# Position table in four rounds of 256 distances, a reordered set-up, and second-layer queries projected in transposed form

## The reference, cut to what matters

```python
# first attention layer
xn = ln(x, g_norm)
q = (xn @ Wq).reshape(b, n, 16, 64).transpose(0, 2, 1, 3)
k, v = split(xn @ Wkv)
k, v = concat(null_kv[0], k), concat(null_kv[1], v)
q, k = l2norm(q) * q_scale, l2norm(k) * k_scale
h = silu(ln(pos @ w0 + b0, g0))        # pos = -n+1 .. n-1
h = silu(ln(h @ w1 + b1, g1))
table = h @ w2 + b2                    # one value for each distance and head
sim = q @ k.T * 8 + table[i - j + n - 1]      # causal, masked
x = x + ln(softmax(sim) @ v @ Wout, g_out)
# second attention layer: no l2norm, scale 1/8, bias read from the input
q = (ln(x, g_in) @ Wq) * 64 ** -0.5
sim = q @ k.T + fside[h, i, j]
x = x + ln(softmax(sim) @ v @ Wo, g_out)
# then two layers: gate, top 2 of 8 experts, two shared experts
logits = (x @ wt.T + (cond @ wg.T)) / 2
```

## Time and profile before

| | us |
|---|---|
| median of the runs | 1698.04 (1697.50 to 1702.49, three runs) |
| the profiled execution, its own time | 1696.38 |
| its span, first to last instruction | 1694.6 |
| PE busy | 1441.5 |
| DVE busy | 1415.4 |
| ACT busy | 1208.0 |
| POOL busy | 775.5 |

### The profile page before, as it was taken

One profiled execution on the slowest core, in us unless ns is written; L12 is line 12 of the kernel. 1 busy time (PEld: TensorE's weight loads), 2 busy tenths in 40 slices (PEclk: granted clock), 3 DMA queues, 4 the chain that ended last, 5 costly groups with the idle time before them and its releaser, 6 DMA issues.

```text
span 1694.6 us, 44574 instructions
## 1 busy us (share of the span) xinstructions
PE 1441.5 (85%) x15543; PEld 1060.4 (63%) x15543; DVE 1415.4 (84%) x3551; ACT 1208.0 (71%) x3063; POOL 775.5 (46%) x1539
## 2 busy tenths in 40 slices
PE   1357777788879999987788888999999989999998
PEld 1245555566667777775566666777777756666665
DVE  4657678888898999986788888899999979888886
ACT  1168788888878999987788888999999923333332
POOL 5657786554444434446664332323222256632222
PEclk9679899999999999998999999999999999999999
DMA  4012121111221123202222121211223001000000
GB/s 141 1 31 63 33 82 51 51 63 64 76 76 67 67 95 111 67 19 59 66 64 68 51 94 70 77 65 72 79 101 130 22 1 44 2 1 1 14 14 26
DMA packets 50496, 96.57 MB, mean 57 GB/s; under 512 B 3396, under 2 KB 27092, under 8 KB 50276
## 3 DMA queue, kind: packets, MB, share of 16 engines
q1 hardware_dynamic: 45568, 90.27, 16.1%
q10 hardware_dynamic: 4708, 3.45, 0.7%
HBM read 91.54 MB, written 2.17 MB: 55 GB/s over the span
## 4 chain that ended last, share of the span: by engine, by line
PE 47%; DVE 19%; ACT 12%; issue 10%; POOL 3%; DMA 1%; DVEq 0%; ACTq 0%; POOLq 0%; SPq 0%
PE tp L1479 7%; DVE p_lo L1105 6%; DVE biased L1019 6%; ACT p_hi L780 5%; PE sc L1186 4%; PE sc L1188 4%; PE sc L1187 4%; PE sc L1373 4%; ACT q_b L709 3%; PE sc L1374 3%; ACT probs L688 2%; PE tp L1186 2%; PE op L1186 2%; PE tp L1187 2%; PE tp L1188 2%
## 5 line engine op out<-in xcount | busy, mean ns | idle before, releaser
L1105 DVE TENSOR_TENSOR p_lo<-tp,p_hi 128x512 f16<-128x512 f32 (+3 forms) x768 | 411.4, 553 | 109.4 <-ACT p_hi L780 102.2
L688 ACT ACTIVATE probs<-biased,neg_max 128x256 f32<-128x256 f32 (+7 forms) x512 | 395.5, 772 | 19.2 <-DVE neg_max L1019 17.8
L1479 PE MATMUL tp<-ident,probs 128*128 128x128 f32 x2304 | 390.3, 279 | 17.9 <-DVE p_lo L1105 16.0
L780 ACT ACTIVATE p_hi<-tp 128x512 f16<-128x512 f32 (+3 forms) x768 | 366.4, 491 | 30.3 <-PE tp L1479 20.8
L1186 PE MATMUL op<-v_s,p_hi 128*128 128x64 f16 x2304 | 285.2, 194 | 55.0 <-DVE p_lo L1105 37.6
L1373 PE MATMUL sc<-k_a,q_a 128*128 128x512 f16 (+3 forms) x768 | 254.3, 331 | 84.1 <-DVE neg_max L1019 75.6
L1479 PEld LDWEIGHTS tp<-ident,probs 128*128 128x128 f32 x2304 | 268.7, 142 | 54.1 <-issue 37.2
L1188 PE MATMUL op<-v_s,p_lo 128*128 128x64 f16 x2304 | 284.2, 194 | 0.0
L1187 PE MATMUL op<-v_s,p_hi 128*128 128x64 f16 x2304 | 284.2, 194 | 0.0
L1186 PEld LDWEIGHTS op<-v_s,p_hi 128*128 128x128 f16 x2304 | 216.2, 99 | 86.9 <-DVE p_lo L1105 62.8
L1374 PE MATMUL sc<-k_b,q_b 128*128 128x512 f16 (+3 forms) x768 | 242.3, 329 | 0.0
(11 more groups left out here) (290 smaller groups left out, 3618.0 us busy)
## 6 DMA issues: line engine op xcount, KB each, us to landing
bias<-rel_table SPq DMA_DIRECT2D x4, 2048.0 KB, 9.0
bias<-in_fside_16xSxS SPq DMA_DIRECT2D x4, 2048.0 KB, 8.3
bias<-rel_table SPq DMA_DIRECT2D x4, 1792.0 KB, 7.3
bias<-in_fside_16xSxS SPq DMA_DIRECT2D x4, 1792.0 KB, 7.6
bias<-rel_table SPq DMA_DIRECT2D x4, 1536.0 KB, 6.2
bias<-in_fside_16xSxS SPq DMA_DIRECT2D x4, 1536.0 KB, 6.5
bias<-rel_table SPq DMA_DIRECT2D x4, 1280.0 KB, 5.6
bias<-in_fside_16xSxS SPq DMA_DIRECT2D x4, 1280.0 KB, 6.1
```

What stands on the lines that cost most here:

```text
L688: ac.activation(probs[:, i % 2, 0:w], biased[:, i % 2, 0:w], ACT.Exp, bias=neg_max[:, u % 2, i % HU:i % HU + 1], scale=-1.0, accum_out=row ...
L780: ac.activation(p_hi[:, gi % 4, 0:nb * P], tp[gi % 2][:, 0:nb * P], ACT.Copy)\
L1105: ve.tensor_tensor(p_lo[:, gi % 4, 0:nb * P], tp[gi % 2][:, 0:nb * P], p_hi[:, gi % 4, 0:nb * P], ALU.subtract).then_inc(s["p_lo"], 1)
L1479: last = te.transpose(tp[gi % 2][:, jj * P:(jj + 1) * P], probs[:, n % 2, (j0 + jj) * P:(j0 + jj + 1) * P], ident[:, :])
```

## The change

Two things are changed together.

The position table is made in four rounds of 256 distances (rounds 0 to 3). Round 0, the distances that tiles 0 and 1 need, is made in slots -18 to -8 (`FILL`). Rounds 1 to 3 are made in slots 0 to 20, 32 to 52 and 64 to 84 (`ROUND`, `ROOTS`), each in small steps inside the attention slots; each writes its quarter of the table, and SP waits for it before the loads of every second tile. The stages are split by operation into `table_stats`, `table_mixed`, `table_scale`, `table_gain`, `table_active` and `table_out` on DVE, `table_tanh` and `table_turned` on ACT, `table_turn` and `table_mix` on PE. What stood before the loop moves into it: x statistics of tile 0 need only x's first tiles, loaded by SP as its first transfer; the null key's products of layer 1 stand at slot -8 behind round 0's table, those of layer 2 are 17 small steps at slots 132 to 148; the gate constants are made at slots 119 and 123 (`PREP`). POOL splits fewer pieces early, in an order that has the first head group first. The null key's logits move from slot 32T-11 to 32T-7, and POOL's null term from unit m+3 to m+2, with two buffers for `q_r`.

In the second layer, queries are projected already transposed: at k = 3, for unit m+2, twelve matmuls of 128 columns with Wq as the fixed operand and x transposed as the moving one. The projection at k = 1, the copy to `q_n` and the two transposes go; the scale moves into the copy to `q_b` and into a scalar_tensor_tensor for the low part.

```diff
-        rh = moe_w[:, 0:2048].rearrange("p (k n) -> p k n", k=TILES)
+        rh = moe_w[:, 0:512].rearrange("p (k n) -> p k n", k=2)
...
-        TABLE_AT = {-17: 4, -15: 5, -14: 6, -10: 7, -8: 8}
+        STATS, SCALE, GAIN, ACTIVE, TURN, MIX, OUT = range(7)
+        FILL = {-18: (STATS, 0), -17: (SCALE, 0), -15: (ACTIVE, 0), -14: (MIX, 0),
+                -10: (SCALE, 1), -9: (ACTIVE, 1), -8: (OUT, 1)}
+        ROUND = {0: (STATS, 0, 0), 1: (STATS, 0, 1), 4: (SCALE, 0, 0), 5: (GAIN, 0, 0), 6: (ACTIVE, 0, 0),
+                 7: (TURN, 0, 0), 8: (MIX, 0, 0), 11: (MIX, 0, 1), 13: (SCALE, 1, 0), 14: (GAIN, 1, 0),
+                 18: (ACTIVE, 1, 0), 19: (TURN, 1, 0), 20: (OUT, 1, 0)}
+        ROOTS = {2: 0, 12: 1}
...
+        PREP = (119, 123)
...
+            sp.dma_start(x_sb[:, :, 0, :], x_in[:, :, 0, :]).then_inc(s_in["x"], 16)
             load_job(sp, 0)
-            load_job(sp, 1)
...
-            write_table(sp)
+            write_table(sp, 0)
             load_bias(sp, 0)
             load_bias(sp, 1)
             n_jobs = 3
             for g in range(2, STEPS * HG):
+                if g % HG == 0 and g <= 3 * HG:
+                    write_table(sp, g // HG)
                 load_bias(sp, g)
...
+            SPLITS = {-17: 2, -16: 2, -15: 2, -13: 1, -9: 1}
...
+                if part == OUT:
+                    table_out(0, sc[1][0:H, 0:2 * P])
+                    null_keys()
...
+            def table_stats(j, i):
+
+                r, half_ = divmod(j, 2)
...
+                    link(ve.scalar_tensor_tensor(rh[:, i, :], rvec[:, 0, :], rel_f[:, k_:k_ + 1], rvec[:, 1, :],
+                                                 ALU.mult, ALU.add))
+                last = ve.bn_stats(r_st[:, i, :], rh[:, i, :])
...
+            def table_scale(j):
+
+                dve.wait_ge(setup["rstd"], j + 1)
+                for i in range(2):
+                    last = ve.tensor_scalar(rh[:, i, :], rh[:, i, :], r_mv[:, i, 0:1], r_rs[:, i:i + 1],
+                                            ALU.subtract, ALU.mult)
+                link(last)
...
+            def table_tanh(j):
+                act.wait_ge(setup["z"], j + 1)
+                ac.activation(re, rh, ACT.Tanh, scale=0.5).then_inc(setup["tanh"], 1)
+
+            def table_turned(j, bank):
+                act.wait_ge(setup["pt"], j + 1)
+                ac.activation(rht.rearrange("p c k n -> p (c k n)"), bank, ACT.Copy).then_inc(setup["t"], 1)
...
+                if k == 3 and U0 <= m + 2 < NU:
+                    u = m + 2
+                    T, hg, bt = u // UNITS, (u % UNITS) // B, u % B
+                    take(False, (s["q_lo"], 2 * (u + 1)))
...
+                    for c in range(UW // P):
+                        cols = slice(hg * UW + c * P, hg * UW + (c + 1) * P)
+                        for kc in range(KC):
+                            last = three(first[:, c * P:(c + 1) * P], wq[1][:, 0, kc, cols], wq[1][:, 1, kc, cols],
+                                         xt[:, T % 2, 0, bt, kc, :], xt[:, T % 2, 1, bt, kc, :],
+                                         kc == 0, kc == KC - 1)
+                    last.then_inc(s["q_t"], 1)
-                if k == 3 and 0 <= m + 2 < NU:
+                if k == 3 and 0 <= m + 2 < U0:
...
-                if k == 1 and 0 <= m + 3 < NU:
+                if k == 1 and 0 <= m + 3 < U0:
```

More of the change, by code:

```diff
@@ L323, in model @@
                 step = min(PIECE, per) if gain is not None else PIECE
-                for c in range(0, size, step):
+                starts = list(range(0, size, step))
+                if gain is not None:
+                    starts.sort(key=lambda c: (c % per, c // per))
+                for c in starts:
                     w = min(step, size - c)
@@ L770, in small @@
                                       ACT.Copy).then_inc(s["ot_hi"], 1)
+                    r, step_ = in_round(n, ROUND)
+                    if r and step_[0] == GAIN:
+                        table_tanh(2 * r + step_[1])
+                    if r and step_[0] == TURN:
+                        table_turned(2 * r + step_[1], second)
                 now = plan.at(n)
@@ L942, in product @@
                                         ALU.mult, ALU.mult).then_inc(f["h"], 1)
-            for p_ in range(3):
-                table_stage(p_)
-            dve.wait_ge(s_in["head"], 16 * HEAD_LOADS)
-            ve.tensor_tensor_reduce(out=null_sq[:, :], in0=null_k[:, :], in1=null_k[:, :], scale=1.0, scalar=0.0,
-                                    op0=ALU.mult, op1=ALU.add, accum_out=null_r[:, :]).then_inc(setup["nss"], 1)
-            link(ve.scalar_tensor_tensor(k_scale[:, :], k_scale[:, :], 8.0, q_scale[:, :], ALU.mult, ALU.mult))
@@ new lines, in gate_prep @@
+            def gate_prep(src):
+                dve.wait_ge(setup["mt"], 1)
+                link(ve.tensor_scalar(wt_f[:, :, :, :].rearrange("p l k e -> p (l k e)"), src[:, 0:32], WS, None, ALU.mult))
+                for l in range(2):
+                    link(ve.tensor_copy(wt_s[:, l, 0, :, :], wt_f[:, l, :, :]))
+                    ve.tensor_tensor(wt_s[:, l, 1, :, :], wt_f[:, l, :, :], wt_s[:, l, 0, :, :], ALU.subtract)
+                ve.tensor_copy(wg_t[:, :, :].rearrange("p l e -> p (l e)"), src[0:G, 32:48])
+                link(ve.tensor_copy(cond_t[:, :], src[0:G, 48:50]))
+                dve.wait_ge(setup["ones"], 1)
+                for b in range(B):
+                    last = ve.tensor_scalar(cond_b[:, b, :], ones64[:, :], cond_t[:, b:b + 1], None, ALU.mult)
+                last.then_inc(setup["cb"], 1)
@@ L1234, in _, with gate_lin @@
+            def gate_lin(bank):
+                pe.wait_ge(setup["cb"], 1)
+                for l in range(2):
+                    for b in range(B):
+                        at_ = (l * B + b) * E
+                        last = te.matmul(bank[:, at_:at_ + E], cond_b[:, b, :], wg_t[:, l, :], start=True, stop=True)
+                last.then_inc(setup["lg"], 1)
+            pe.wait_ge(setup["ident"], 1)
             free = {0: [], 1: [], 2: []}
@@ L1441, in small @@
                                                  kc == 0, kc == KC - 1)
+                            last.then_inc(s["kv"], 1)
+                        if n == n0 - 7:
+                            take(True, (s["k_lo"], T + 1), (s["null_t"], T + 1))
+                            if layer == 0:
+                                pe.wait_ge(s["k_dup"], T + 1)
+                            for bt in range(B):
+                                last = te.transpose(second[:, bt * P:(bt + 1) * P], k_d[:, bt, :], ident[:, :])
                             if t == 0:
-                                pe.wait_ge(s["wnk"], KC * (layer + 1))
-                            if layer == 0:
-                                pe.wait_ge(s["xr_lo"], T + 1)
+                                pe.wait_ge(s["wnk"], layer + 1)
                             x_q = xr if layer == 0 else xt[:, T % 2]
                             for bt in range(B):
-                                at_ = B * 2 * DH + bt * H
+                                at_ = B * P + bt * H
                                 for kc in range(KC):
@@ L1452, in small @@
                                                  kc == 0, kc == KC - 1)
-                            last.then_inc(s["kv"], 1)
-                        if n == n0 - 7:
-                            take(True, (s["k_lo"], T + 1))
-                            if layer == 0:
-                                pe.wait_ge(s["k_dup"], T + 1)
-                            for bt in range(B):
-                                last = te.transpose(second[:, bt * P:(bt + 1) * P], k_d[:, bt, :], ident[:, :])
                             last.then_inc(s["kt"], 1)
```

522 lines of the change are left out of this document (298 added, 224 removed).

## The result

The changed kernel takes 1709.97 us (median of four runs, 1708.70 to 1711.58) where the kernel before takes 1697.77 (1697.43 to 1702.49): 1.0065 times the time before, 95% interval 1.0053 to 1.0077. The forecast was 1676, with 1654 to 1692 as its range. Slower had been given 0.07.

A forecast was written before the change was run, and what follows sets the result against it. Three regimes were taken to bound it: a serial set-up, latency-bound early slots, and full PE and DVE in the last tile. The terms -44.6 + 32 + 3.5 - 1 - 11 = -21.1 gave 1676 us, range 1654 to 1692.

The forecast's parts named there:

- term E: Second-layer query projection: 0.15 us gained per narrow unit and 0.2 per wide unit, -11 us (-22 to +3).
- all of that work is worth 0.35: Wide layer-2 units: a tile 7 unit without projection and copy took 11.66 us against 12.01; the change gives back 0.2.
- the delay at k = 3 counts everywhere: Second-layer queries, worst case: q_b's later start is paid everywhere and DVE takes the gain, a loss of 3 us.
- term B: Table rounds 1 to 3 inside the first layer's slots: 10.7 us each, +32 us (+15 to +42).
- less half for cover: Plain DVE steps of the rounds (statistics, scaling, last product): 5.2 us a round, half hidden, leaving 2.6.
- the second rival: Set-up and rounds: POOL leads, set-up -36 us and rounds +38, total 1691.5 us; chance 0.13.
- term A: Set-up: first bias addition at 47.5 us instead of 92.15, -44.6 us (-50 to -36).
- term C: Gate constants made at slots 119 and 123, PE and DVE waiting for each other: +3.5 us (2 to 5).
- term D: Second layer's null key, two lumps of some 2.6 us turned into 17 small steps: -1 us (-4 to +1).
- the query change does nothing or harm, rounds dear: Rival on second-layer queries and table rounds: rounds +42 us, queries +3, total 1701 us; chance 0.08.
- POOL leads: Same as the second rival: set-up -36 us, rounds +38, queries still -11, total 1691.5 us; chance 0.13.

The follow-up runs named there:

- setup_fast: Changed kernel with the gain column loaded first on ACT's queue, masks first on SP's, mask conversions ahead of the weight pieces: 1706.25 us.
- table_only: Changed kernel with the old second-layer queries put back, so the new table alone: 1700.27 us, ratio 1.0003 to the kernel before.
- best: Changed kernel with setup_fast's edits, round consumers a slot later, transposed projection ahead of the scores only in layer 2's first four tiles: 1676.25 us.
- no_rounds: Changed kernel without rounds 1 to 3, the table's other three quarters filled with round 0's values: 1671.23 us.

## Why the prediction was wrong, step by step

**Second-layer queries (term E, -11; measured +11.8 by tiles, +8.3 alone).** The decisive step, with the wrong sign. The delay of 0.44 us of q_b at k = 3 was seen, and then netted against the 0.4 to 0.66 us gained at k = 1, as if both had the same price, which left a gain of 0.15 and 0.2 a unit. The runs give them different prices. Of 0.55 us taken away at k = 1 only 0.19 (by tiles) to 0.22 come back, since the next wait takes the rest; of 0.44 us put in at k = 3, 0.33 to 0.38 are paid. For the wide tiles I read 12.01 and 11.66 (rows 8) as "all of that work is worth 0.35". That row told what removing a projection gives, 0.35, and nothing of what a delay ahead of ACT's chain costs; here the same measure after is 11.94 for every unit, the last too (timeline of ACT, kernel after):

```profile
1324.43 0.63 ACT L759 ACTIVATE q_a<-q_b 64x512 f16<-64x512 f16 x1
1336.37 0.63 ACT L759 ACTIVATE q_a<-q_b 64x512 f16<-64x512 f16 x1
1348.31 0.63 ACT L759 ACTIVATE q_a<-q_b 64x512 f16<-64x512 f16 x1
```

The bound +3, for the case that "the delay at k = 3 counts everywhere", was too mild as well. The delay in full is 64 x 0.44 = 28, so a loss of 3 leaves a gain of 25, and the gain at the measured price is 17. What was right: twelve matmuls of 128 columns take 0.66 us (the tenth starts 0.50 behind the first in the timeline above), and DVE's scaled subtraction costs the same 0.88 for two.

**Rounds (term B, +32; measured +38.7).** The mechanism was right, the size was off, inside its bounds (15 to 42). The mis-sized terms: the tanh's wait was 2.3 us on average (13.6 / 6) where the whole hand-over had been put at 1.5; and DVE's own steps cost 5.7 of their 8 us a round, about 0.3 of them covered, where "less half for cover" had been taken off the plain ones. In tile 0 part of it may be another thing that I hadn't priced: PE's granted clock (see below). The port that DVE and GpSimd share was weighed as the second rival, and it did stretch steps of the rounds. The two scalings of a step took 0.73 us together in tile 0 and 1.50 in tile 1, beside POOL (timelines, kernel after):

```profile
72.13 0.73 DVE L900 TENSOR_SCALAR moe_w<-moe_w,r_mv,r_rs 128x256 f32<-128x256 f32 x2
...
144.40 0.72 POOL L639 TENSOR_TENSOR y_acc<-y_acc,g_out 128x256 f32<-128x256 f32 x1
...
144.58 1.50 DVE L900 TENSOR_SCALAR moe_w<-moe_w,r_mv,r_rs 128x256 f32<-128x256 f32 x2
...
145.21 0.73 POOL L641 TENSOR_TENSOR x<-x,y_acc 128x256 f32<-128x256 f32 x1
```

Six of the twelve scalings and two of the six first products of the rounds are longer in this way, 3.1 us in all over the shortest of their kind, or 1 us a round; the six gains took 0.68 to 0.76. So the port is a small part of the 38.7.

**Set-up (term A, -44.6; measured -36.2).** At its outer bound, -36. The gain column's landing (14.6 us) was missing from the chain, which put the first root 3 us late, and the mask conversion took another 1.7 us from DVE's product. Both were found and mended in setup_fast, for 3.7 us; 4.8 us are left there, and the largest piece found is POOL's wait of 2.93 us for Wq, which the forecast had at nothing.

**Gate constants (term C, +3.5).** Tile 3 is longer by 5.6 after, by 2.2 in table_only and best, by 3.8 in no_rounds. The bounds 2 to 5 nearly hold it; why it varies between kernels that don't differ there stays open.

**Null key of layer 2 (term D, -1).** Tiles 4 and 5 together -4.5: better than its bound of -4.

**The rivals.** The nearest was the one with "the query change does nothing or harm, rounds dear", 1701 at a chance of 0.08. Its queries' +3 and set-up's -44.6 were both too kind. *POOL leads* had A at -36 and B at +38, nearly what was measured, and kept E at -11; in the set-up POOL did lead (its late roots, its conversion), in the rounds it cost DVE about 1 us each. Each of the three large terms missed to the same side: 8.4, 6.7 and 23 us, where the range let them offset each other. They don't have one cause: A missed loads that landed late and a blocked product, B and E the price of a step that is put into a chain of in-order engines.

**What to carry over.** Price an insertion and a removal differently: find what stands behind the new instruction on the engine that waits for it, and count a delay there nearly in full (0.33 to 0.38 us of 0.44 here), also where the profile shows idle time; count a removed wait at half (12.3 to 13.8 us of 24.4). When a step of another chain is put into a pipelined loop, issue its consumer a slot later than its producer on the next engine: the same work cost 13 us less. And ask for each width of slot, since the place that was right for narrow tiles (0.62 us of idle PE ahead of the scores) brought nothing in tiles 4 and 5 and was wrong for the two widest.
